# A graph network on one core: attention prepared further ahead, 32 row buffers, and one field shared between VectorE and ScalarE

## The reference

```python
h = relu(layernorm(x))
fwd = segment_sum(w[:, None] * h[dst, :128], src) / clip(deg_src, 1)     # first half of the features
bwd = segment_sum(w[:, None] * h[src, 128:], dst) / clip(deg_dst, 1)     # second half
x = x + concat(fwd, bwd)
h = relu(layernorm(x))
# eight attention heads of 64, then one of 256; one such layer is:
#   z = h @ W.T + b;  e = exp(-leaky_relu(z[src] @ a1 + z[dst] @ a2))
#   out = layernorm(segment_sum(e[:, None] * z[dst], src)) * g + beta;  elu
out = x + elu(head_out(concat(elu(head_i(h)) for i in range(8))))
```

## Time and profile before

| | |
|---|---|
| runs | 3130.0, 3130.86, 3134.51 us (median 3130.86) |
| the profiled execution | 3138.38 us, its span 3136.6 us |
| granted TensorE clock, mean | 0.849 |
| busy, share of the span | PE 76%, PE weight loads 58%, DVE 69%, ACT 51%, POOL 65% |

### The profile page before, as it was taken

How to read it: one execution, slowest core, us unless ns; L and a number is a source line. 1 busy time by engine, 2 the same in 40 slices (tenths; PEclk the granted TensorE clock), 3 DMA queues, 4 the chain that set the end, 5 groups by cost and what they waited for, 6 DMA issues and landing times. The chain is left out here.

```text
span 3136.6 us, 48973 instructions
## 1 busy us (share of the span) xinstructions
PE 2368.6 (76%) x16450; PEld 1814.2 (58%) x16450; DVE 2162.2 (69%) x4446; ACT 1589.7 (51%) x4526; POOL 2049.6 (65%) x2003
## 2 busy tenths in 40 slices
PE   1777689888898789875667788888884677777761
PEld 1677688878888688853334444444443555555551
DVE  9999888878887698843226588888877433434337
ACT  0454466656665566643333445545547555555544
POOL 1010277777777777777774577777766477777772
PEclk7999899989999799975558899999996887887775
DMA  2001011111112411122226577777780233333352
GB/s 63 1 1 43 16 46 45 45 47 47 46 47 46 49 45 45 44 58 51 51 52 82 175 209 209 210 208 210 208 181 8 74 107 105 106 106 106 106 96 57
DMA packets 114891, 270.64 MB, mean 86 GB/s; under 512 B 34543, under 2 KB 51670, under 8 KB 114646
## 3 DMA queue, kind: packets, MB, share of 16 engines
q0 software_dynamic: 89088, 245.53, 31.4%
q1 hardware_dynamic: 25558, 21.98, 2.1%
HBM read 250.96 MB, written 16.42 MB: 85 GB/s over the span
## 5 line engine op out<-in xcount | busy, mean ns | idle before, releaser
L388 POOL DMA_INDIRECT rows_near<-table_a,s_idx_S x464 | 534.8, 1153 | 227.5 <-issue 112.5
L1039 DVE TENSOR_TENSOR work<-work,bank 128x129 f32 (+2 forms) x928 | 390.4, 421 | 302.9 <-PE bank L725 208.7
L388 POOL DMA_INDIRECT rows_near<-table_b,s_idx_D x464 | 500.0, 1078 | 141.4 <-issue 105.4
L388 POOL DMA_INDIRECT rows_near<-table,s_idx_S x464 | 446.7, 963 | 173.6 <-issue 124.3
L388 POOL DMA_INDIRECT given<-table,s_idx_S x464 | 448.0, 965 | 141.3 <-issue 124.6
L725 PE MATMUL bank<-rows_near,oh 128*128 128x129 f32 x1856 | 385.3, 341 | 180.8 <-ACT rows_near L497 146.9
L711 PE MATMUL bank<-scratch 128*128 128x224 bf16 (+1 forms) x2520 | 401.7, 270 | 110.2 <-DVE scratch L1014 77.4
L841 PE MATMUL bank<-scratch,oh 128*128 128x512 f32 x928 | 448.7, 629 | 21.3 <-DVE scratch L1197 21.3
L711 PE MATMUL bank<-rows_near,sort_ring 128*128 128x224 bf16 (+1 forms) x2520 | 403.0, 271 | 68.4 <-ACT sort_ring L488 39.8
L725 PEld LDWEIGHTS bank<-rows_near,oh 128*128 128x128 f32 x1856 | 295.2, 227 | 258.4 <-ACT rows_near L497 189.8
L580 ACT ACTIVATE e_att<-lrelu 128x32 f32<-128x32 f32 (+1 forms) x232 | 50.4, 217 | 606.0 <-DVE lrelu L1186 606.0
(11 more groups left out here) (198 smaller groups left out, 4431.3 us busy)
## 6 DMA issues: line engine op xcount, KB each, us to landing
rows_near<-table_a,s_idx_S POOLq DMA_INDIRECT x464, 2.7
rows_near<-table_b,s_idx_D POOLq DMA_INDIRECT x464, 2.7
rows_near<-table,s_idx_S POOLq DMA_INDIRECT x464, 3.6
given<-table,s_idx_S POOLq DMA_INDIRECT x464, 3.6
table<-scratch SPq DMA_DIRECT2D x25, 260.0 KB, 2.1
table<-scratch SPq DMA_DIRECT2D x25, 128.5 KB, 2.9
xs<-in_x SPq DMA_DIRECT2D x1, 3072.0 KB
out_x<-scratch SPq DMA_DIRECT2D x24, 128.0 KB, 1.7
```

What stands on the lines that cost most here:

```text
L388: nc.gpsimd.indirect_dma_start(out=to, out_offset=None, in_=table[:, :], in_offset=bass.IndirectOffsetOnAxis(ap=s_idx[order][:, c:c + 1], ...
L1039: v.tensor_add(a, a, psum).then_inc(sum_free[o], 1)
```

## The change

- **Part 0 of the sort.** Of the ten columns of `oh_i1`, ACT makes four (`ACT_COLS`), with a float copy of the half index that POOL makes (`half_f`); DVE makes six. Parts 1 to 3 are as they were.
- **Layer 0.** 32 row buffers (16 more in `scratch2`, whose column of ones DVE sets), 8 sums in four banks in place of 6 in three, DVE adds three quads behind instead of two until the first tile is complete.
- **First dense product.** Turned tiles alternate between banks 0 and 1, the scores of a block stand in the same bank, and DVE waits for both tiles of a block before it takes the first. The stage buffers move to `scratch`.
- **Attention.** One-hots are made six quads ahead, turned five, scored three; the order is written out for all 116 quads. ACT copies the source scores from PSUM to SBUF (`s_edge`), so that DVE's score add has both operands in SBUF. Eight quads of one-hots, four of turned ones, three of messages, sums in six banks; DVE adds two quads behind instead of one.
- **Attention 2.** 32 row buffers. Attention 1 keeps 16.

```diff
+ACT_COLS = 4
+ROWS0 = 2 * SLOTS
+ROWS2 = 2 * SLOTS
+OH_QUADS = 8
+OHT_QUADS = 4
+SUMS = 6
+AHEAD = {"oh": 6, "turn": 5, "evict": 4, "score": 3}
...
# POOL
-                    pool.wait_ge(chunks_summed, phase * CHUNKS + c + 1)
-                    gather(table, rows0[:, c % SLOTS, 0:HALF], order, c)
+                    n = phase * CHUNKS + c
+                    if n == SLOTS:
+                        pool.wait_ge(rows_made, 1)
+                    if n >= ROWS0:
+                        pool.wait_ge(chunks_summed, n + 1 - ROWS0)
+                    gather(table, row0(n)[:, 0:HALF], order, c, gathered[n % ROWS0])
...
-                    elif c >= SLOTS:
-                        pool.wait_ge(sum_ready[o], (c - SLOTS) // GP + 1)
+                    elif c >= ROWS2 and o == "2":
+                        pool.wait_ge(sum_ready[o], (c - ROWS2) // GP + 1)
...
                 g.tensor_copy(half_index[o], both(bits[0]))
+                if o == "S":
+                    g.tensor_copy(half_f, bits[0])
...
# ACT
+                    if part == 0 and j < ACT_COLS:
+                        last = nc.scalar.activation(oh_i1[n % RING][:, j, :], oh_lane[n % RING][:, j, :], ACT.Copy,
+                                                    scale=half_f[:, c:c + 1])
                 last.then_inc(fields_ready, 1)
...
+                def evict(turn, score):
+                    act.wait_ge(turn_psum[o], turn + 1)
+                    if turn < QUADS:
+                        nc.scalar.activation(ohT[:, turn % OHT_QUADS, :], turned[turn % 2], ACT.Copy).then_inc(ohT_ready[o], 1)
+                    if 0 <= score < QUADS:
+                        if score >= 4:
+                            act.wait_ge(z_ready[o], score - 3)
+                        n = QUAD * heads
+                        nc.scalar.activation(s_edge[:, score % 4, 0:n], selected[score % 2][:, 0:n], ACT.Copy).then_inc(ssrc_ready[o], 1)
...
+                for q in range(-AHEAD["oh"], QUADS):
+                    if 0 <= q + 1 < QUADS:
+                        weights(q + 1)
+                    turn = q + AHEAD["evict"]
+                    if 0 <= turn < QUADS + AHEAD["turn"] - AHEAD["score"]:
+                        evict(turn, turn + AHEAD["score"] - AHEAD["turn"])
+                    if q + AHEAD["oh"] < QUADS:
+                        one_hots(q + AHEAD["oh"])
...
# PE, attention: per step turn quad q + 5 and score quad q + 3, then
+                        last.then_inc(turn_psum[o], 1)
+                    if q >= 0:
+                        sums(q)
...
# DVE
-                v.tensor_tensor(two(oh_i1[slot]), two(oh_lane[slot]), along(half_index[o], P), ALU.mult).then_inc(col_ready, 1)
+                skip = ACT_COLS if part == 0 else 0
+                v.tensor_tensor(two(oh_i1[slot][:, skip:, :]), two(oh_lane[slot][:, skip:, :]), along(half_index[o], P, skip),
+                                ALU.mult).then_inc(col_ready, 1)
...
+            v.memset(more_rows0[:, :, HALF:HALF + 1], 1.0).then_inc(rows_made, 1)
...
                 if 0 <= n - 4 < len(BLOCKS):
+                    dve.wait_ge(dense_psum["1"], BLOCKS[n - 4].stop)
                     for t in BLOCKS[n - 4]:
                         dense("1", HD, HEADS, s_src1, tab_1, t)
...
-                                    bank[2 + u % 2][:, 0:n].rearrange("p (k h) -> p k h", h=heads),
-                                    row_slots(u % UNROLL * QUAD, QUAD)[:, :, width:width + heads], ALU.add).then_inc(z_ready[o], 1)
+                                    s_edge[:, q % 4, 0:n].rearrange("p (k h) -> p k h", h=heads),
+                                    row_slots(o, q * QUAD, QUAD)[:, :, width:width + heads], ALU.add).then_inc(z_ready[o], 1)
...
+                for q in range(QUADS + 2):
+                    if q < QUADS:
+                        messages(q)
+                    if q + 1 < QUADS:
+                        scores(q + 1)
+                    if q >= 2:
+                        add_groups(q - 2, tiles[q % 4 * 2:q % 4 * 2 + 2])
```

More of the change, by code:

```diff
@@ L75, in build @@
         turned = [bank[i][:, 0:QUAD * P // 2].bitcast(BF16) for i in range(2)]
+        selected = [bank[i][:, QUAD * P // 2:QUAD * P // 2 + QUAD * HEADS] for i in range(2)]
         table_a = nc.dram_tensor("table_a", (T * P, HALF), F32, kind="Internal").ap()
@@ L137, in build @@
         s_src2 = sb("s_src2", [P, T, 1])
-        s_rest = [scratch[:, 9 * HD + i * T * HEADS:9 * HD + (i + 1) * T * HEADS].rearrange("p (t h) -> p t h", h=HEADS) for i in range(2)]
         given = sb("given", [P, 15, COLS])
@@ L143, in build @@
         nat_w = given[:, 2, :]
+        half_f = given[:, 2, :]
         def pairs(row, dt):
@@ L221, in build, with after_gains @@
         gains = sort_ring[:, 0:3 * (HD + C)]
-        s_parts = sort_ring[:, 3 * (HD + C):3 * (HD + C) + 3 * T * HEADS // 2].bitcast(BF16).rearrange("p (f t h) -> p f t h", f=3, h=HEADS)
+        behind = 3 * (HD + C)
+        def after_gains(n):
+            nonlocal behind
+            behind += n
+            return sort_ring[:, behind - n:behind]
+        s_parts = after_gains(3 * T * HEADS // 2).bitcast(BF16).rearrange("p (f t h) -> p f t h", f=3, h=HEADS)
+        s_rest = [after_gains(T * HEADS).rearrange("p (t h) -> p t h", h=HEADS) for i in range(2)]
+        s_edge = after_gains(4 * QUAD * HEADS).rearrange("p (a c) -> p a c", a=4)
         cols, cols_neg = gains[:, 0:8], gains[:, 8:16]
@@ L272, in build @@
         tab_2 = [sem(f"tab_2{i}") for i in range(2)]
-        gathered = [sem(f"gathered{i}") for i in range(SLOTS)]
+        gathered = [sem(f"gathered{i}") for i in range(ROWS0)]
+        rows_made = sem("rows_made")
         chunks_summed = sem("chunks_summed")
@@ L384, in _, with gather @@
             nc.gpsimd.memset(work[:, :, C:HD], 0.0).then_inc(acc_zeroed, 1)
-            def gather(table, to, order, c):
+            def gather(table, to, order, c, landed):
                 nc.gpsimd.indirect_dma_start(
@@ L844, in sums @@
                             mm.then_inc(sum_ready[o], 1)
-                def turn(i):
-                    n = 2 * UNROLL if not isinstance(i, int) or i < ROUNDS - 1 else 2 * UNROLL - 2
-                    tiles = tile_numbers(mybir.EngineType.PE, "S", i * (2 * UNROLL) + (TILE_AT + 2), n)
-                    for u in range(UNROLL):
-                        q = i * UNROLL + u
-                        if not isinstance(i, int) or q + 1 < QUADS:
-                            source_scores(i * UNROLL + (u + 1), u + 1, tiles[2 * u:2 * u + 2])
-                        if not isinstance(i, int) or q + 2 < QUADS:
-                            transposed(i * UNROLL + (u + 2), u + 2)
-                        sums(q, u)
-                transposed(0, 0)
-                transposed(1, 1)
-                source_scores(0, 0, tile_numbers(mybir.EngineType.PE, "S", TILE_AT, 2))
-                turn(0)
-                for i in range(1, ROUNDS - 1):
-                    turn(i)
-                turn(ROUNDS - 1)
+                for q in range(-AHEAD["turn"], QUADS):
+                    turn, score = q + AHEAD["turn"], q + AHEAD["score"]
+                    if score >= 0 and score % 4 == 0 and score < QUADS:
+                        tiles = tile_numbers(mybir.EngineType.PE, "S", TILE_AT + 2 * score, min(8, GROUPS - 2 * score))
+                    if score < QUADS:
+                        if turn >= 2 and turn < QUADS + 2:
+                            pe.wait_ge(ohT_ready[o], turn - 1)
+                        if score >= 2:
+                            pe.wait_ge(ssrc_ready[o], score - 1)
+                        if turn < QUADS:
+                            last = transposed(turn)
+                        if score >= 0:
+                            last = source_scores(score, tiles[score % 4 * 2:score % 4 * 2 + 2])
+                        last.then_inc(turn_psum[o], 1)
+                    if q >= 0:
+                        sums(q)
             pe.wait_ge(dense_dve["1"], T)
```

206 lines of the change are left out of this document (101 added, 105 removed).

## The result

The changed kernel takes 3140.86 us (median of 8 runs, 3136.11 to 3148.54) where the kernel before takes 3130.47 beside it (8 runs, 3127.19 to 3136.03): a ratio of 1.003, 95% interval 1.0018 to 1.0043. The forecast was 3121.2, range 3112 to 3130. The time is 11 us above the range, and on the other side of no change.

A forecast was written before the change was run, and what follows sets the result against it. The prediction took POOL's chain of gathers, lengthened by DVE but never waiting for buffers, as the bound; -11.1 + 0.9 + 0.5 = -9.7 us took the median 3130.86 to 3121.2 us, range 3112 to 3130.

The forecast's parts named there:

- Part 0, -11.1: Sort, part 0: four columns fewer on DVE in each of 42 batches bring the first gather earlier, -11.1 us.
- Rival 3: Sort, part 0: DVE's cost is fixed or ACT's copies end last, so only +1.4 us is left, 3132; chance 0.07.
- Layer 0, 0 with 4 either way: Layer 0: more buffers, more sums and later adds remove waits POOL does not have; 0, with 4 us either way.
- Dense product, +0.9: First dense product: DVE waits for both tiles of a block, so the last table row is late; +0.9 us, between 0.7 and 2.2.
- Rival 5: Stretch from phase D to attention 1: the landing wait of 7.30 us moves either way, 3114 or 3128; chance 0.07.
- Attention's start: Start of both attentions: first exponential 4 to 7 us later, covered by row buffers; without cover up to 7 us once.
- Attention's loop, 0: Attention loop: an added ACT copy per quad and fewer TensorE waits lie off POOL's path; 0 us.
- rival 1: Attention 1's message blocks: DVE lengthens more gathers, 31 us in place of 15, giving 3137; chance 0.07.
- Rival 4: Attention 1: the lengthening of gathers goes, 15 us more gained, giving 3106; chance 0.07.
- Score add, 0: Attention loop: DVE's score add with both operands in SBUF could lengthen gathers; between 0 and 53 us, taken as 0.
- rival 2: Attention loop: the score adds hold up gathers by 5 us, giving 3126; chance 0.10.
- The ends, +0.5: Ends of both attentions: two more adds stand behind the last messages; +0.5 us together, between 0 and 3.

The follow-up runs named there:

- e1: The kernel before plus only the sort's part 0 change (ACT makes four of ten columns, DVE six): 3125.29 us, ratio 0.9960.
- a1: The changed kernel run again, unaltered: 3146.22 us against 3136.92 for the kernel before, ratio 1.0026.
- e2: The changed kernel without its part 0 change (ACT_COLS set to 0): 3158.58 us, ratio to the kernel before 1.0063.
- e3: The changed kernel with DVE's attention loads of tile numbers moved back one quad, to words 2, 10, 18 as before: 3140.22 us, ratio to before 1.0005.
- e14: The kernel before with DVE's attention loads of eight tile numbers taken from words 4 + 8i instead of 2 + 8i: 3145.67 us, ratio 1.0020.
- e11: The changed kernel with each layer-0 phase's first tile-number load put back between the one-hots of quads 0 and 1: 3137.37 us, ratio to before 0.9998.
- e13: The kernel before with each layer-0 phase's first tile-number load moved behind the one-hots of quad 3, ahead of the first add: 3143.66 us, ratio 1.0018.
- e12: The changed kernel with both repairs, the early first layer-0 load and the attention loads at words 2, 10, 18: 3123.48 us, ratio to before 0.9952.
- e7: The changed kernel with layer 0's sums added two quads behind throughout, as before: ratio to before 1.0077, on a chip where the kernel before takes about 3494 us.
- e4: The kernel before with DVE's attention loads taken from words 4 + 8i instead of 2 + 8i, on a slow chip: ratio 1.0007.
- e9: The kernel before with DVE's attention loads from words 4 + 8i instead of 2 + 8i, run again on a slow chip: ratio 1.0029.

## Why the prediction was wrong, point by point

- **What bounds the kernel** (POOL's chain of gathers, no wait for buffers): held. No wait of POOL inside a phase is over 0.3 us after the change either, on chips like the one shown.
- **Part 0, -11.1**: held. The first gather comes 11.25 us earlier, e1 is 11.6 faster. L1069, `oh_i1`, took 0.54 us in place of 0.82, and a batch 250.33 - 243.90 = 6.43 us where 6.42 was forecast. **Rival 3** fell with it.

```profile
243.90 0.80 DVE L1062 TENSOR_TENSOR scratch<-iota_lane,given 128x1280 bf16<-128x1280 bf16 x1
...
248.07 0.54 DVE L1069 TENSOR_TENSOR scratch<-scratch,given 128x768 f16<-128x768 bf16 x1
...
250.33 0.80 DVE L1062 TENSOR_TENSOR sort_ring<-iota_lane,given 128x1280 bf16<-128x1280 bf16 x1
```

- **Layer 0, 0 with 4 either way**: this is the first step that failed. The text said that the removed waits, POOL having none, cost "nothing", and that only the general lengthening could move by 4 us. One gather of 12.5 us put 11.6 back (12.53 less 0.945), and S grew by 13.3 (mean of the changed kernel, a1, e2, e3: 687.0; of before, e1, e14: 673.7). The cause is a step that the text did not cost: the register load of tile numbers moved from between the first one-hots to ahead of the first add, and e11 and e13 move the long gather with it. D went the other way by 3.7 us (634.5 in the same four, 638.2 in before, e1, e13, e14). No run isolates that gain; e11 and e12, with the early load, have 637.7 and 636.2.
- **Dense product, +0.9**: held. Before, DVE took the last tile at 1742.94 and the first gather came 3.14 us later, at 1746.08. Now it takes the last two together at 1736.14, and the first gather comes 3.91 us later, at 1740.05: 0.77 more.

```profile
1736.14 0.69 DVE L1186 TENSOR_TENSOR scratch<-bank,sort_ring 128x512 f32<-128x512 f32 x1 [4.08 <-PE bank L800]
...
1736.89 0.68 DVE L1186 TENSOR_TENSOR scratch<-bank,sort_ring 128x512 f32<-128x512 f32 x1
```

  The whole stretch from the last gather of D to the first of attention 1 scatters by more than that: 65.9 to 68.5 us before (before, e1, e13, e14) and 67.4 to 68.8 after (changed, a1, e2, e3, e11). **Rival 5** asked for 7 us there, and fell.
- **Attention's start**: hidden, as said, but not as described. The first exponential was to come 12 to 15 us behind the first gather and came 8.6 behind (before 8.1). Before, ACT had stood idle for 3.11 us ahead of it; that idle time took up added work, which the sum of ACT's pieces had overlooked.

```profile
1748.69 0.23 ACT L649 ACTIVATE e_att<-lrelu 128x32 f32<-128x32 f32 x1
```

- **Attention's loop, 0**: the second step that failed, by 11.6 us (604.9 in changed, a1, e2 and e11 against 593.3). The term listed ACT's copy and TensorE's waits and left out DVE's own pause, though the text read the same 100 us in which it stands. Seeing 82 of 100 us busy on DVE in the earlier trace rows, it did not ask what the rest was. The mechanism was that of **rival 1** (0.07): the messages lengthen more gathers. Taken gather by gather from the two traces, 92 took 1.00 us or more against 53, and what they took above 0.945 us is 24.5 us against 14.5. All of them started inside a block of messages. That is 0.21 us a quad, just the point at which that rival was said to decide. What the rival lacked was the cause. **Rival 4** (less lengthening) had the sign wrong.

  The prediction's reading of the earlier trace rows, that a gather which starts inside a block takes 1.31 us, holds for a part of them only. 226 gathers before and 227 after start inside a block of 2.5 us, two in nearly each. Those that start over 1.25 us behind its first message were never lengthened (113 before, 114 after). Of the 113 that start earlier in it, 53 were lengthened before and 92 after. From 0.75 to 1.00 us behind the first message, 15 started before and 35 after, and all of these were lengthened. So the messages do not meet more starts; the starts have moved within the block.

  TensorE's idle time behind ACT's one-hots did not vanish but grew, from 56.8 us to 72.2, at no cost. In rows of before and after:

```profile
PE bank L816 <- ACT oh L571: 56.8, 83, 2.2
```

```profile
PE bank L872 <- ACT oh L633: 36.6, 51, 2.3
PE bank L872 <- ACT given L633: 35.6, 43, 3.0
```

- **Score add, 0**: held, and **rival 2** fell. Of the 92 lengthened gathers none overlaps L1245. A quad of the changed kernel, DVE and POOL side by side, answers to the earlier trace rows:

```profile
2312.75 2.50 DVE L1260 TENSOR_TENSOR scratch<-rows_near,e_att 128x512 f32<-128x512 f32 x4
2316.19 0.19 DVE L1245 TENSOR_TENSOR score<-sort_ring,rows_near 128x32 f32<-128x32 f32 x1 [0.94 <-DMA rows_near<-table,s_idx_S]
```

```profile
2313.45 1.41 POOL L438 DMA_INDIRECT given<-table,s_idx_S  x1 [0.30 <-DVE scratch L1260]
2315.16 0.94 POOL L438 DMA_INDIRECT given<-table,s_idx_S  x1 [0.30 <-issue]
2316.41 0.94 POOL L438 DMA_INDIRECT given<-table,s_idx_S  x1 [0.30 <-issue]
```

  The score follows a landing, and its 0.19 us fall ahead of the next gather's start at 2316.41. By the rule of the Trainium skill that the prediction cites, the sum would have carried 5 us; this trace shows none of it, as the operation misses the starts.
- **The 32 buffers, 0**: held. Attention 2 lasted 581.3 us before and 581.7 after.
- **The ends, +0.5**: too small to tell. From attention 1's last gather to attention 2's first it took 138.6 to 140.4 us (before, e1, e13, e14) and 137.7 to 140.1 (changed, a1, e2, e3, e11).
- **The sum.** -11.2 (part 0) + 13.3 (S) - 3.7 (D) + 1.1 (the stretch behind it) + 11.6 (attention 1) - 0.3 (the stretch behind that) + 0.6 (attention 2), by the means over these profiles, is +11.4 us, against +10.4 by the medians of the result and +9.3 by a1's. The range failed because both failed terms stood at zero with no bound beyond 4 us, though lengthening was named as the only thing that makes the gathers' time.

## What to carry to other kernels

Where one engine's chain of equal steps sets the time and another engine lengthens them, an edit that moves that other engine by a tenth of a microsecond can be on the path (here 0.10 us between two one-hots went with 11.6 us): cost it with a range of both signs, and measure part by part. Read the waits that end in "issue" on the engine that interferes, and look at its queue for register loads, before calling a reordering free. Take such a change apart: here a few lines of it (e1) held nearly the whole gain.

## What the runs showed of the hardware that was not expected

- **A register load's length goes with its address.** Eight words from 0, 8, 16 and so on, or from 4, 12, 20 (e14, and layer 0 after), take 0.60 us on DVE's queue, from 2, 10, 18 they take 1.84 (e3, e14: the loads moved both ways). From 6, 14, 22 they took 1.94 on TensorE's queue, from 4, 12, 20 after the change 0.59; no run moves these alone. The first load of DVE in the program takes 0.84 to 0.85 from word 0 or 4. In the attention DVE's data path stands still for 1.23 of the 1.84. The Trainium skill ("DMA: Bandwidth & Descriptors", section "Latency and other measured facts") gives about 600 ns as the floor of such a load. Most of the even loads agree, but not all: in before, phase D's first load, of eight words from word 0, took 0.35 us.
- **A gather can be shut out across many instructions of DVE.** Begun at 356.81 in e3, it ended at 369.34, and fifteen DVE instructions ran in that time; in e7 and e13 it took 7.5 us, until DVE first waited. The Trainium skill ("SBUF — State Buffer", section "Who interferes with whom") calls the port pair that the two engines share an exclusive lock, held by whoever issues first for the whole instruction; the latter it says of DVE's two-port modes. Read so for these operations, the wait would be bounded by one of them, 1.4 us at most here; the runs show more. Why only a gather at this place is shut out, when those of e11 get through nearly the same run of DVE (1.44 and 1.03 us), was not settled; that the early load decides it was shown in both kernels. Whether it does so by the 0.10 us that it sets the one-hots apart was not tested.
- **Chips differ.** On two of the chips used the kernel before takes 3494 us; the kernel before with the even load (e4, e9) has POOL waiting for buffers in attention 1 there. Five variants of the changed kernel took 0.8 to 2% longer than the kernel before; the changed kernel itself did not run there. The profiles say where the variants lose. S lasts 738 to 753 us in them against 720.5 in e4 and 720.6 in e9, with one wait of POOL of 20.6 to 24.9 us for the merge of part 1 (3.3 in e4), and the stretch between D and attention 1 is 74 to 78 us against 61.3. In attention 1 the four with the even load gain: 732 to 745 against 759 and 765. Why the merge comes late there was not looked into.
